# Layer normalisation phases in four groups of four batches, half of the normalising on GpSimd in five of the eight

## The chip, the cores and the metric

The kernel runs on one core of one Trainium2 chip. The metric is the time of one execution in microseconds, measured on the device; lower is better. Times of a profile come from one profiled execution.

## The reference

Input is `x` of 16 batches x 112 rows x 256 features and a context of 16 x 375 x 256, all float32. Four layers follow, each an attention over the context and a feed-forward part with eight experts. Each of the eight parts reads a layer normalisation of the running `x` and is added to it:

```python
def _layernorm(x, axis=-1, eps=1e-05):
    m = jnp.mean(x, axis=axis, keepdims=True)
    v = jnp.var(x, axis=axis, keepdims=True)
    return (x - m) / jnp.sqrt(v + eps)
...
    x = x + _L0_xattn_ref(ctx_1024, _layernorm(x, axis=-1), ctx_1024, ...)
    x = x + _L0_ffn_ref(_layernorm(x, axis=-1), ...)
    x = x + _L1_xattn_ref(_layernorm(x, axis=-1), ctx_1024, ...)
    x = x + _L1_ffn_ref(_layernorm(x, axis=-1), ...)
    x = x + _L2_xattn_ref(_layernorm(x, axis=-1), ctx_1024, ctx_1024, ...)
    x = x + _L2_ffn_ref(_layernorm(x, axis=-1), ...)
    x = x + _L3_xattn_ref(_layernorm(x, axis=-1), ctx_1024, ctx_1024, ...)
    x = x + _L3_ffn_ref(_layernorm(x, axis=-1), ...)
    return x
```

The parts differ: softmax attention with 16 heads of 16 features (layers 0 and 3) or 64 (layer 2), a linear attention (layer 1), and experts chosen by one or two winners or weighted by gates. The change touches only what computes `_layernorm`.

## The kernel before

`x` lies in SBUF as the tile `X` for the whole run: 112 rows on the partitions, 16 batches of 256 features. Each of the eight parts is a phase function that opens with a call of `layernorm_phase` (L95). The calls, by the tag that names their tiles in the trace (the tile of the normalised rows is `a0n_xn` and so on, or `d_xn` in the routers r1, r5 and r7 of the sparse feed-forward parts): a0 and a6 from `narrow_attention_phase` (L833), a2 from `linear_attention_phase` (L1198), a4 from `attention_phase` with heads of 64 (L320), and r1, r3, r5, r7 from `router_phase` (L1552).

`layernorm_phase` is one block of all five engines, with a barrier of all engines at its end (L43), and makes `XT`, the normalised rows turned so that features lie on the partitions. Within it:

- VectorE (DVE) works in two halves of eight batches: `bn_stats` of each batch (L126), `bn_aggr` of each (L129), for both halves; then for each half a `reciprocal` of the eight roots (L133) and eight `tensor_scalar` that subtract the mean and multiply (L138), each 112x256.
- ScalarE (ACT) takes a root of each half's variances (L155) and then copies the eight PSUM banks out to `XT` (L160), each 128x448.
- TensorE (PE) turns each batch in two halves of 128 features (L170), four batches to a bank: for each group of four the four first halves, each waiting for its batch, and then the four second halves. So there are 32 transposes and 8 banks.
- SyncE (SP) runs `fetch`, the DMA of what the phase behind needs: weights, biases, the first context tiles.
- GpSimd (POOL) runs `prepare` where a caller gives one: in a0 and a6 it fills `k`, `q` and `values` (L829 to L831), in a2 one small tile (L1196). `attention_phase` passes a `prepare` as well, but its body does something only with heads of 16, which a4 hasn't. The routers pass none.

The order on each engine is the order of the code; engines meet by semaphores. An instruction that waits holds all that stands behind it on its engine. After the barrier of a4 the first instruction of ScalarE that counts is the cast of a context tile that DMA brings (L467), behind a wait for all weights; ScalarE's casts of the weights and its evacuation of the first projections follow it.

Of the kernel before, what the change touches and what calls it, by code (L numbers as in the profile page):

```python
# [9 lines left out]
ALU = mybir.AluOpType  # L10
ACT = mybir.ActivationFunctionType
AX = mybir.AxisListType

B, S, D = 16, 112, 256
# [4 lines left out]
GT = 4  # L19
G = B // GT  # L20
# [73 lines left out]

def layernorm_phase(nc, tag, X, XT, ident, xn=None, fetch=None, prepare=None):  # L95


    HB = B // 2
    with ExitStack() as st:
        m = Mem(nc, st, tag)  # L100
        stats = m.sb("stats", [S, B, 6])
        mean_var = m.sb("mean_var", [S, B, 2])
        eps = m.sb("eps", [S, 1])
        warm = m.sb("warm", [S, 1])
        std = m.sb("std", [S, B])
        rstd = m.sb("rstd", [S, B])
        xn = m.sb("xn", [S, B, D]) if xn is None else xn
        banks = [m.bank(f"b{i}") for i in range(8)]
        stats_done, mv_done, std_done, rstd_done = (m.sem(n) for n in ("stats", "mv", "std", "rstd"))
        xn_done, turned, evacuated, eps_done = (m.sem(n) for n in ("xn", "turned", "evac", "eps"))  # L110
        with nc.Block() as block:
            if fetch is not None:
                @block.sync
                def _(sp):
                    fetch(sp)

            if prepare is not None:
                @block.gpsimd
                def _(pool):
                    prepare(pool)  # L120

            @block.vector
            def _(dve):
                def statistics(i):
                    for b in range(i * HB, (i + 1) * HB):
                        dve.bn_stats(stats[:, b, :], X[:, b, :]).then_inc(stats_done, 1)  # L126
                    dve.wait_ge(stats_done, (i + 1) * HB)
                    for b in range(i * HB, (i + 1) * HB):
                        dve.bn_aggr(mean_var[:, b, :], stats[:, b, :]).then_inc(mv_done, 1)  # L129

                def invert(i):
                    dve.wait_ge(std_done, i + 1)
                    dve.reciprocal(rstd[:, i * HB:(i + 1) * HB], std[:, i * HB:(i + 1) * HB]).then_inc(rstd_done, 1)  # L133

                def normalise(i):
                    dve.wait_ge(rstd_done, i + 1)
                    for b in range(i * HB, (i + 1) * HB):
                        dve.tensor_scalar(xn[:, b, :], X[:, b, :], mean_var[:, b, 0:1], rstd[:, b:b + 1],  # L138
                                          ALU.subtract, ALU.mult).then_inc(xn_done, 1)

                dve.memset(eps[:, :], LN_EPS).then_inc(eps_done, 1)
                statistics(0)
                statistics(1)
                invert(0)
                normalise(0)
                invert(1)
                normalise(1)

            @block.scalar
            def _(act):  # L150
                act.wait_ge(eps_done, 1)
                act.activation(warm[:, :], eps[:, :], ACT.Sqrt)
                for i in range(2):
                    act.wait_ge(mv_done, (i + 1) * HB)
                    act.activation(std[:, i * HB:(i + 1) * HB], mean_var[:, i * HB:(i + 1) * HB, 1], ACT.Sqrt,  # L155
                                   bias=eps[:, 0:1]).then_inc(std_done, 1)
                for g in range(G):
                    for c in range(DC):
                        act.wait_ge(turned, g * DC + c + 1)
                        act.copy(XT[:, c, g * GW:(g + 1) * GW], banks[g * DC + c][:, 0:GW]).then_inc(evacuated, 1)  # L160
                act.wait_ge(evacuated, G * DC)

            @block.tensor
            def _(pe):
                for g in range(G):
                    for c in range(DC):
                        for t in range(GT):
                            if c == 0:
                                pe.wait_ge(xn_done, g * GT + t + 1)
                            mm = pe.transpose(banks[g * DC + c][:, t * S:(t + 1) * S],  # L170
                                              xn[:, g * GT + t, c * 128:(c + 1) * 128], ident[0:S, 0:S])
                        mm.then_inc(turned, 1)


def attention_phase(nc, tag, X, XT, ident, ctxT, Wq, Wk, Wo, bo, bq=None, bk=None, Wv=None, bv=None,
# [9 lines left out]
    HB = 128 // step  # L185
# [20 lines left out]
    with ExitStack() as st:  # L206
        m = Mem(nc, st, tag)
# [20 lines left out]
        if mask is not None:  # L228
# [11 lines left out]
        projected, evacuated = m.sem("projected"), m.sem("evacuated")  # L240
        scored, least_done, exp_done, inv_done, P_done = (
            m.sem(n) for n in ("scored", "least", "exp", "inv", "P_done"))
        turned, PT_done, av_done, y_done, out_done, x_done = (
            m.sem(n) for n in ("turned", "PT_done", "av", "y", "out", "x_done"))
# [32 lines left out]
        def load_keys(sp, b, u):  # L277
            sp.dma_start(kc[:, u, :, :], ctxT[b].rearrange("(c p) s -> p c s", p=128)).then_inc(kc_in[u], 16)

        def load_rest(sp, b, u):  # L280

            if ctx is not None:
                if not (isinstance(b, int) and b < 2):
                    sp.wait_ge(av_done, H * (b - 1))
                sp.dma_start(v[:, u, :, :], ctx[b].rearrange("(j p) d -> p j d", p=KP)).then_inc(v_in[u], 16)
            if mask is not None:
                src = mask[b] if mask_kind == "per_query" else mask[b].to_broadcast([S, SK])
                sp.dma_start(mask_raw[:, u, :], src).then_inc(mask_in[u], 16)
# [25 lines left out]
        def prepare(pool):  # L314
            if hd == 16:
                pool.memset(wo[:, :, :], 0.0).then_inc(zeroed, 1)
                pool.memset(q[:, :, :, :, :], 0.0).then_inc(zeroed, 1)
                pool.memset(k[:, :, :, :], 0.0).then_inc(zeroed, 1)

        layernorm_phase(nc, tag + "n", X, XT, ident, fetch=fetch, prepare=prepare)  # L320
        P = m.sb("P", [S, 4, SK])
        PT = m.sb("PT", [KP, 2 * HB, KT, S])
        yT = m.sb("yT", [128, 2, NB, S])
# [8 lines left out]
        with nc.Block() as block:  # L332
            @block.sync
            def _(sp):
                def stack(b, u):

                    if not (isinstance(b, int) and b < 2):
                        sp.wait_ge(stack_in[u], 16 * NSLOT * (b // 2) if isinstance(b, int) else (b - u) * (8 * NSLOT))
                        sp.sem_inc(sp_waited, 1)
                    sp.wait_ge(parts_made, QK * (b + 1))  # L340
                    rows = lambda d: d[u].rearrange("n (c p) s -> p n c s", p=128)
                    for part in range(2):
                        sp.dma_start(rows(q_dram)[:, part], q_parts[:, part, :, :]).then_inc(parts_out, 16)
# [36 lines left out]
                stack(B - 1, 1)  # L380
# [1929 lines left out]
```

## Time and profile before

| what | value |
|---|---|
| three runs | 3030.3, 3033.42, 3039.56 us; median 3033.42 |
| the profiled execution | 3027.69 us |
| its span | 3026.1 us, 59465 instructions |
| PE busy | 2436.0 us (81%) |
| DVE busy | 1298.1 us (43%) |
| ACT busy | 1126.1 us (37%) |
| POOL busy | 953.0 us (31%) |
| all `tensor_scalar` of L138 | 128, in eight phases of 16 |

Busy time is a share of the whole span; what a phase costs is read in the timeline of that phase, from its first `bn_stats` to its last copy of L160.

### The profile page before, as it was taken

How to read it: one execution, taken by the hardware profiler on the slowest of the kernel's cores; microseconds unless marked ns; L12 is line 12 of the kernel's file. 1: busy time of each engine (PE TensorE's matmuls, PEld its weight loads, DVE VectorE, ACT ScalarE, POOL GpSimd, SP SyncE). 2: the span in 40 equal slices, each digit the busy share in tenths (PEclk: the TensorE clock that was granted, in tenths of full speed). 3: DMA queues.
4: the chain of work that ended last, by engine and by line, in shares of the span. 5: the costliest groups of instructions: out<-in, count | busy, mean ns of one | idle time of the engine just before them, and what ended most of it. 6: DMA issues, size and time to landing. Idle time of an engine off the chain costs nothing. (4 is left out here: it accounts for less than half of the span.)

```text
span 3026.1 us, 59465 instructions
## 1 busy us (share of the span) xinstructions
PE 2436.0 (81%) x20918; PEld 1782.1 (59%) x20918; DVE 1298.1 (43%) x3094; ACT 1126.1 (37%) x2531; POOL 953.0 (31%) x1201
## 2 busy tenths in 40 slices
PE   3998499499999999879799899899865962899653
PEld 1555289366777776646466666666634851555432
DVE  4555401445554555435344444444451224544432
ACT  1455143333333333121455555555421211455411
POOL 4332200344333344100345444544333025222022
PEclk9899599799999999979899999999976986999867
DMA  6552198200000000000564565565404633332045
GB/s 168 102 104 63 43 324 309 97 17 12 7 12 12 12 12 2 2 11 18 137 124 98 98 129 103 94 125 109 75 15 153 219 127 88 72 67 62 6 128 164
DMA packets 334154, 266.26 MB, mean 88 GB/s; under 512 B 128376, under 2 KB 314624, under 8 KB 333952
## 3 DMA queue, kind: packets, MB, share of 16 engines
q1 hardware_dynamic: 324112, 237.70, 32.8%
q0 software_dynamic: 9840, 25.70, 2.5%
q8 instruction: 146, 2.39, 0.4%
q14 instruction: 56, 0.46, 0.1%
HBM read 181.19 MB, written 57.61 MB: 79 GB/s over the span
## 5 line engine op out<-in xcount | busy, mean ns | idle before, releaser
L1292 POOL TENSOR_TENSOR a_kp<-a_kp 125x512 f16<-125x512 f32 x192 | 219.0, 1158 | 394.7 <-ACT a_kp L1321 384.5
L993 DVE TENSOR_REDUCE a_mx<-a_s 112x2 f32<-112x750 f32 x256 | 234.5, 935 | 224.3 <-PE a_s L1050 224.2
L1420 PE MATMUL a_u<-a_wkf,a_kc 128*125 128x512 f16 x1152 | 263.0, 389 | 27.5 <-issue 20.0
L395 POOL TENSOR_SCALAR a_P<-a_P,a_inv 112x375 f32<-112x375 f32 x256 | 151.7, 593 | 357.3 <-DVE a_inv L555 355.8
L550 DVE CUSTOM_DVE_ANT_0 a_masked<-a_s,a_mask_add 112x375 f32<-112x375 f32 x256 | 140.1, 547 | 281.4 <-PE a_s L661 279.8
L475 ACT ACTIVATE a_P<-a_masked,a_least 112x375 f32<-112x375 f32 x256 | 156.0, 609 | 200.9 <-DVE a_least L550 198.6
L1420 PEld LDWEIGHTS a_u<-a_wkf,a_kc 128*125 128x125 f16 x1152 | 158.7, 140 | 121.3 <-issue 36.0
L945 ACT ACTIVATE a_PT<-a_x 125x672 f32<-125x672 f32 x256 | 186.8, 730 | 100.4 <-PE a_x L1063 99.0
L2115 ACT ACTIVATE f_h<-f_h,f_b1s 128x128 f32<-128x128 f32 (+1 forms) x294 | 116.4, 397 | 240.2 <-PE f_h L2089 227.5
L1342 DVE TENSOR_SCALAR a_kp<-a_u 125x512 f32<-125x512 f32 x192 | 128.5, 689 | 179.4 <-PE a_u L1420 146.8
L561 DVE COPY a_PT<-a_t 125x336 f32<-125x336 f32 x256 | 129.1, 504 | 153.2 <-PE a_t L670 153.2
L1321 ACT CAST a_kp<-a_kp 125x512 f16<-125x512 f32 x192 | 117.8, 618 | 193.7 <-DVE a_kp L1342 193.7
L2089 PE MATMUL f_h<-f_xT,f_w 128*128 128x128 f32 (+1 forms) x1176 | 183.7, 313 | 0.1
L2100 PE MATMUL f_o<-f_w,f_h 128*128 128x256 f32 x756 | 174.1, 381 | 0.0
L2089 PEld LDWEIGHTS f_h<-f_xT,f_w 128*128 128x128 f32 x1176 | 165.1, 197 | 9.7 <-ACT f_h L2115 0.4
L634 PE MATMUL a_p<-a_kc,a_wk 128*128 128x375 f16 x768 | 143.8, 325 | 29.0 <-ACT a_raw L456 29.0
L2043 POOL DMA_DIRECT2D expert_rows<-f_y x63 | 38.0, 602 | 385.7 <-DVE f_y L2132 385.3
L2132 DVE COPY f_y<-f_o 128x256 f32<-128x256 f32 x84 | 35.7, 425 | 279.5 <-PE f_o L2100 279.5
L2100 PEld LDWEIGHTS f_o<-f_w,f_h 128*128 128x128 f32 x756 | 141.6, 192 | 17.3
L637 PE MATMUL a_p<-a_wv,a_kc 128*125 128x512 f16 x576 | 140.8, 383 | 0.0
L661 PE MATMUL a_s<-a_k,a_q 128*112 128x375 f16 x512 | 129.2, 336 | 9.1 <-DMA a_k<-k_parts 8.9
L670 PEld LDWEIGHTS a_t<-all_ident,a_P 112*125 112x125 f32 x768 | 118.9, 192 | 17.8 <-POOL a_P L395 2.2
(316 smaller groups left out, 4822.2 us busy)
## 6 DMA issues: line engine op xcount, KB each, us to landing
f_w<-in_L_ffn_W SPq DMA_DIRECT2D x42, 1024.0 KB, 6.6
a_kc<-in_ctxT SPq DMA_DIRECT2D x64, 375.0 KB, 5.0
k_parts<-a_k_parts SPq DMA_DIRECT2D x32, 750.0 KB, 7.3
a_k<-k_parts SPq DMA_DIRECT2D x32, 750.0 KB, 11.3
f_w<-in_L_ffn_ew SPq DMA_DIRECT2D x42, 512.0 KB, 3.8
a_k<-a_k_parts SPq DMA_DIRECT2D x192, 93.8 KB
a_q<-q_parts SPq DMA_DIRECT2D x64, 224.0 KB, 4.6
f_w<-in_L_ffn_W SPq DMA_DIRECT2D x42, 256.0 KB, 3.0
```

The lines of the kernel that those rows point to most:

```text
L395: pool.tensor_scalar(P[:, h % 4, :], P[:, h % 4, :], inv[:, u, h:h + 1], 1.0, ALU.mult, ALU.mult).then_inc(P_done, 1)
L475: act.activation(P[:, h % 4, :], src, ACT.Exp, bias=least[:, u, h:h + 1], scale=-1.0, accum_out=total[:, u, h:h + 1]).then_inc(exp_done, 1)
L550: dve.tensor_tensor_reduce(masked[:, h % 2, :], s_bank[h % 2][0:S, 0:SK], mask_add[:, u, :], 1.0, 3e38, ALU.add, ALU.min, least[:, u, h:h ...
L634: mm = pe.matmul(out[:, 0:SK], wk16[:, z, i, c * 128:(c + 1) * 128], kc16[:, u, x, i, :], **flags)
L637: mm = pe.matmul(out[0:KP, 0:VN], kc16[:, u, x, i, c * KP:(c + 1) * KP], wv16[:, z, i, w * VN:(w + 1) * VN], **flags)
L661: mm = pe.matmul(s_bank[h % 2][0:S, 0:SK], q[:, u, NPASS - 1 - n, h, :], k[:, u, h * KH // H, :], start=n == 0, stop=n == NPASS - 1)
L945: act.activation(PT[:, p % 4, :, :], x_bank[0:KP, :, 0:KT * S], ACT.Exp).then_inc(exp_done, 1)
L993: dve.tensor_reduce(mx[:, b % 2, 2 * pair:2 * pair + 2], s_bank[p % 2][0:S, :, 0:SK], AX.X, ALU.max).then_inc(max_done, 1)
L1292: pool.tensor_tensor(kp16[:, LO, j, w * 512:(w + 1) * 512], kp[:, n % 4, :], kp16[:, HI, j, w * 512:(w + 1) * 512], ALU.subtract).then_inc ...
L1420: mm = pe.matmul(out[0:KP, 0:512], kc16[:, u, a, c, j * KP:(j + 1) * KP], wt[:, z, c, w * 512:(w + 1) * 512], start=n_mm == 0, stop=n_mm = ...
L2089: mm = pe.matmul(h_bank[n % R][:, 0:TS], w1[:, s, c, f * 128:(f + 1) * 128], xT[:, s, c, :], start=c == 0, stop=c == DC - 1)
L2100: mm = pe.matmul(o_bank[n % R][:, 0:D], h[:, s, f, t * 128:(t + 1) * 128], w2[:, s, f, :], start=f == 0, stop=f == FC - 1)
```

## The change

The statistics, inversion and normalising go in four groups of four batches instead of two halves of eight. VectorE computes statistics one group ahead of the normalising. In a phase without `prepare` VectorE normalises the first two batches of each group and GpSimd the other two; with `prepare`, VectorE normalises all four. ScalarE takes the root of group g before it copies the banks of group g - 2. PE waits for VectorE's or GpSimd's semaphore according to the batch. `attention_phase` passes its `prepare` only with heads of 16, so that in a4 GpSimd shares in the normalising; r1, r3, r5 and r7 do as well, a0, a2 and a6 don't.

```diff
+    own = GT if prepare is not None else 2
...
+        def normalise(eng, b, done):
+            eng.tensor_scalar(xn[:, b, :], X[:, b, :], mean_var[:, b, 0:1], rstd[:, b:b + 1],
+                              ALU.subtract, ALU.mult).then_inc(done, 1)
...
+            @block.gpsimd
+            def _(pool):
+                if prepare is not None:
                     prepare(pool)
+                else:
+                    for g in range(G):
+                        pool.wait_ge(rstd_done, g + 1)
+                        for t in range(own, GT):
+                            normalise(pool, g * GT + t, xn_pool)
...
+                def statistics(g):
+                    for b in range(g * GT, (g + 1) * GT):
                         dve.bn_stats(stats[:, b, :], X[:, b, :]).then_inc(stats_done, 1)
+                    dve.wait_ge(stats_done, (g + 1) * GT)
+                    for b in range(g * GT, (g + 1) * GT):
                         dve.bn_aggr(mean_var[:, b, :], stats[:, b, :]).then_inc(mv_done, 1)
...
+                def invert(g):
+                    dve.wait_ge(std_done, g + 1)
+                    dve.reciprocal(rstd[:, g * GT:(g + 1) * GT], std[:, g * GT:(g + 1) * GT]).then_inc(rstd_done, 1)
+                    dve.wait_ge(rstd_done, g + 1)
+                    for t in range(own):
+                        normalise(dve, g * GT + t, xn_dve)
...
                 statistics(0)
-                statistics(1)
-                invert(0)
-                normalise(0)
-                invert(1)
-                normalise(1)
+                for g in range(1, G):
+                    statistics(g)
+                    invert(g - 1)
+                invert(G - 1)
...
+                for g in range(G):
+                    act.wait_ge(mv_done, (g + 1) * GT)
+                    act.activation(std[:, g * GT:(g + 1) * GT], mean_var[:, g * GT:(g + 1) * GT, 1], ACT.Sqrt,
+                                   bias=eps[:, 0:1]).then_inc(std_done, 1)
+                    if g >= 2:
+                        evacuate(g - 2)
+                evacuate(G - 2)
+                evacuate(G - 1)
...
+                            if c == 0 and t < own:
+                                pe.wait_ge(xn_dve, g * own + t + 1)
+                            elif c == 0:
+                                pe.wait_ge(xn_pool, g * (GT - own) + t - own + 1)
...
-        layernorm_phase(nc, tag + "n", X, XT, ident, fetch=fetch, prepare=prepare)
+        layernorm_phase(nc, tag + "n", X, XT, ident, fetch=fetch, prepare=prepare if hd == 16 else None)
```

## Rows read from the trace of the kernel before

**Rows 1.** Timeline of r1: start us, us, engine, line, operation, count, idle before and releaser.
```profile
309.97 0.43 DVE L126 BATCH_NORM_STATS2 r1n_stats<-all_X 112x6 f32<-112x256 f32 x1 [1.20 <-PEq L43]
...
313.27 2.68 DVE L126 BATCH_NORM_STATS2 r1n_stats<-all_X 112x6 f32<-112x256 f32 x8
...
316.55 0.17 DVE L133 RECIPROCAL r1n_rstd<-r1n_std 112x8 f32<-112x8 f32 x1
...
316.75 2.68 DVE L138 TENSOR_SCALAR d_xn<-all_X,r1n_mean_var,r1n_rstd 112x256 f32<-112x256 f32 x8
...
317.22 6.65 PE L170 MATMUL r1n_b<-all_ident,d_xn 112*128 112x112 f32 x32 [8.92 <-DVE d_xn L138]
...
323.16 0.53 ACT L160 COPY all_XT<-r1n_b 128x448 f32<-128x448 f32 x1 [0.21 <-PE r1n_b L170]
323.90 0.53 ACT L160 COPY all_XT<-r1n_b 128x448 f32<-128x448 f32 x1 [0.22 <-PE r1n_b L170]
```

**Rows 2.** Timeline of r3, then stretches: us, PE busy (count), granted clock, DMA share, GB/s.
```profile
1282.25 2.71 DVE L126 BATCH_NORM_STATS2 r3n_stats<-all_X 112x6 f32<-112x256 f32 x8
...
1294.94 0.97 ACT L160 COPY all_XT<-r3n_b 128x448 f32<-128x448 f32 x2 [0.17 <-PE r3n_b L170]
...
1291.00:1292.00 1.00, 1.00 (x7) 0.50 0.00 0
...
1294.00:1295.00 1.00, 0.99 (x9) 1.00 0.00 0
```

**Rows 3.** Timeline of a2.
```profile
568.17 2.71 DVE L126 BATCH_NORM_STATS2 a2n_stats<-all_X 112x6 f32<-112x256 f32 x8
...
579.86 1.99 ACT L160 COPY all_XT<-a2n_b 128x448 f32<-128x448 f32 x4 [0.21 <-PE a2n_b L170]
```

**Rows 4.** Timeline of a0.
```profile
16.57 10.10 POOL L829 MEMSET a_k<- 128x12000 f16 x1 [14.82 <-POOLq L43]
...
19.95 2.68 DVE L126 BATCH_NORM_STATS2 a0n_stats<-all_X 112x6 f32<-112x256 f32 x8
...
23.43 13.90 DVE L138 TENSOR_SCALAR a0n_xn<-all_X,a0n_mean_var,a0n_rstd 112x256 f32<-112x256 f32 x8
...
26.61 6.22 POOL L830 MEMSET a_q<- 128x7168 f16 x1
...
26.87 0.45 PE L170 MATMUL a0n_b<-all_ident,a0n_xn 112*128 112x112 f32 x1 [26.87 <-DVE a0n_xn L138]
32.77 2.79 POOL L831 MEMSET a_values<- 125x3072 f32 x1
...
35.77 5.59 PE L170 MATMUL a0n_b<-all_ident,a0n_xn 112*128 112x112 f32 x30 [2.29 <-DVE a0n_xn L138]
...
37.47 2.68 DVE L138 TENSOR_SCALAR a0n_xn<-all_X,a0n_mean_var,a0n_rstd 112x256 f32<-112x256 f32 x8
...
41.01 0.97 ACT L160 COPY all_XT<-a0n_b 128x448 f32<-128x448 f32 x2 [0.18 <-PE a0n_b L170]
```

**Rows 5.** Timeline of a6.
```profile
2540.24 2.68 DVE L138 TENSOR_SCALAR a6n_xn<-all_X,a6n_mean_var,a6n_rstd 112x256 f32<-112x256 f32 x8
...
2542.33 2.08 ACT L160 COPY all_XT<-a6n_b 128x448 f32<-128x448 f32 x4 [0.21 <-PE a6n_b L170]
```

**Rows 6.** GpSimd operations by line: min/median/max ns; the last from the groups: busy us, mean ns.
```profile
L395 POOL TENSOR_SCALAR a_P<-a_P,a_inv x256: 591/592/602, 1515.7 to 2198.3; 112x375 f32<-112x375 f32 x128
...
L921 POOL TENSOR_SCALAR a_bqT<-a_bqT x2: 277/386/496, 42.9 to 2545.3; 128x2 f32<-128x2 f32 x2
...
L1564 POOL TENSOR_TENSOR all_X<-all_X,d_xn 112x256 f32<-112x256 f32 x16 | 11.0, 723 | 23.3 <-SPq L1559 23.3
```

**Rows 7.** Timeline of a4 and what follows.
```profile
1446.84 0.43 DVE L126 BATCH_NORM_STATS2 a4n_stats<-all_X 112x6 f32<-112x256 f32 x1 [0.99 <-PEq L43]
...
1460.77 0.53 ACT L160 COPY all_XT<-a4n_b 128x448 f32<-128x448 f32 x1 [0.21 <-PE a4n_b L170]
...
1462.95 0.82 ACT L467 CAST a_kc<-a_kc 128x750 f16<-128x750 f32 x1 [1.65 <-DMA a_kc<-in_ctxT]
```

More of the change, by code:

```diff
@@ L95, in layernorm_phase @@
 def layernorm_phase(nc, tag, X, XT, ident, xn=None, fetch=None, prepare=None):
-    HB = B // 2
+    own = GT if prepare is not None else 2
     with ExitStack() as st:
@@ L109, in layernorm_phase @@
         stats_done, mv_done, std_done, rstd_done = (m.sem(n) for n in ("stats", "mv", "std", "rstd"))
-        xn_done, turned, evacuated, eps_done = (m.sem(n) for n in ("xn", "turned", "evac", "eps"))
+        xn_dve, xn_pool, turned, evacuated, eps_done = (m.sem(n) for n in ("xn_dve", "xn_pool", "turned", "evac", "eps"))
+        def normalise(eng, b, done):
+            eng.tensor_scalar(xn[:, b, :], X[:, b, :], mean_var[:, b, 0:1], rstd[:, b:b + 1],
+                              ALU.subtract, ALU.mult).then_inc(done, 1)
         with nc.Block() as block:
@@ L115, in _ @@
                     fetch(sp)
-            if prepare is not None:
-                @block.gpsimd
-                def _(pool):
+            @block.gpsimd
+            def _(pool):
+                if prepare is not None:
                     prepare(pool)
+                else:
[3 more added lines that the diff above has]
+                            normalise(pool, g * GT + t, xn_pool)
             @block.vector
@@ L123, in _ @@
             def _(dve):
-                def statistics(i):
-                    for b in range(i * HB, (i + 1) * HB):
+                def statistics(g):
+                    for b in range(g * GT, (g + 1) * GT):
                         dve.bn_stats(stats[:, b, :], X[:, b, :]).then_inc(stats_done, 1)
-                    dve.wait_ge(stats_done, (i + 1) * HB)
-                    for b in range(i * HB, (i + 1) * HB):
+                    dve.wait_ge(stats_done, (g + 1) * GT)
+                    for b in range(g * GT, (g + 1) * GT):
@@ L129, in statistics @@
                         dve.bn_aggr(mean_var[:, b, :], stats[:, b, :]).then_inc(mv_done, 1)
[L131 to L139, printed above, removed]
+                def invert(g):
[4 more added lines that the diff above has]
+                        normalise(dve, g * GT + t, xn_dve)
@@ L141, in _ @@
                 dve.memset(eps[:, :], LN_EPS).then_inc(eps_done, 1)
                 statistics(0)
-                statistics(1)
-                invert(0)
-                normalise(0)
-                invert(1)
-                normalise(1)
+                for g in range(1, G):
+                    statistics(g)
+                    invert(g - 1)
+                invert(G - 1)
             @block.scalar
             def _(act):
-                act.wait_ge(eps_done, 1)
-                act.activation(warm[:, :], eps[:, :], ACT.Sqrt)
@@ L153, in _, with evacuate @@
[L153 to L157, printed above, removed]
+                def evacuate(g):
                     for c in range(DC):
@@ L160, in _ @@
                         act.copy(XT[:, c, g * GW:(g + 1) * GW], banks[g * DC + c][:, 0:GW]).then_inc(evacuated, 1)
+                act.wait_ge(eps_done, 1)
+                act.activation(warm[:, :], eps[:, :], ACT.Sqrt)
+                for g in range(G):
[6 more added lines that the diff above has]
+                evacuate(G - 1)
                 act.wait_ge(evacuated, G * DC)
@@ L167, in _ @@
                         for t in range(GT):
-                            if c == 0:
-                                pe.wait_ge(xn_done, g * GT + t + 1)
+                            if c == 0 and t < own:
+                                pe.wait_ge(xn_dve, g * own + t + 1)
+                            elif c == 0:
+                                pe.wait_ge(xn_pool, g * (GT - own) + t - own + 1)
                             mm = pe.transpose(banks[g * DC + c][:, t * S:(t + 1) * S],
```

## Prediction

> **What bounds the kernel now.** The page's first part comes first: PE is by far the busiest engine, so a stretch in which PE stands still costs its full length. The eight layer normalisations are such stretches: each stands alone between two barriers of all engines, and what follows it starts only when its last ScalarE copy is done. I call them by their tags: a0, r1, a2, r3, a4, r5, a6, r7. I read each in the timeline, counted from the first `bn_stats` of VectorE (DVE).
>
> r1 [rows 1] is the plain case. Eight `bn_stats` and eight `bn_aggr` take 313.27 to 316.55 = 3.28 us, 2.68 of it the `bn_stats`; the aggregates are 0.07 each. A `reciprocal` is followed by the first normalising `tensor_scalar` 0.20 us later. Eight of those take 316.75 + 2.68; one lasts 0.41 us and follows the last by 0.324 us. The first comes at 6.78 us, the sixteenth ends at 12.28. PE then transposes 32 times in 6.65 us without a gap; the last copy ends at 323.90 + 0.53, that is at 14.46. a4 repeats the pattern to the same end. In r3, r5 and r7 the last copy ends at 13.66 (1294.94 + 0.97 - 1282.25 in r3, which stands for the three): the granted clock of PE is 0.50 at first and 1.00 in the last microsecond [rows 2]. 1.00 is the 2.4 GHz level and 0.50 the 1.2 GHz level. a2 ends at 579.86 + 1.99 - 568.17 = 13.68 [rows 3].
>
> a0 and a6 differ. GpSimd fills three large tiles there (10.10, 6.22 and 2.79 us). DVE's `bn_stats` run at their usual pace beside the first (8 in 2.68), but the first `tensor_scalar`, issued at 23.43, has its result only when PE starts at 26.87, 0.2 us after the first memset ends at 26.67. The second and third likewise come out at the ends of the second and third memset: PE's long run starts at 35.77 [rows 4]. So a DVE `tensor_scalar` and a GpSimd instruction exclude each other, and a `bn_stats` doesn't care. In a0 DVE then needs until 37.47 + 2.68 = 40.15 and the copies until 41.01 + 0.97 = 41.98 [rows 4]; in a6 2540.24 + 2.68 = 2542.92 and 2542.33 + 2.08 = 2544.41 [rows 5].
>
> **The change part by part.** First the units. Statistics of four batches instead of eight: 3.28 less four spacings (1.30) and four aggregates (0.28) = 1.70 us. Inversion and n normalisations: 0.20 + 0.324 n. The tail from the last normalised batch to the last copy, when PE isn't behind: 0.06 to wake, five transposes at 0.186 (four in 0.74, the spacing of the last copies [rows 1]), 0.2 to drain, 0.03 + 0.53 for the copy = 1.75 us; at the higher clock half the transposing, about 1.3.
>
> *a0 and a6, four batches on DVE: a loss.* DVE is in order. It now comes to its first `tensor_scalar` at about 3.6 us, while the first memset runs on to 26.67, and there it stands: the statistics of groups 2 and 3, which before lay under that memset, are queued behind it. The three releases stay where they are, since the memsets set them. The fourth `tensor_scalar` starts at 23.43 + 13.90 - 0.41 - 4 x 0.324 = 35.62 [rows 4] and frees DVE at 35.95. Then statistics 1.70, group 1 1.50, statistics 1.70, group 2 1.50, and group 3 with 0.20 + 3 x 0.324 + 0.41: the last ends at 43.93 in place of 40.15, 3.78 us later. With the tail of 1.75 the last copy ends at 45.68 instead of 41.98: +3.7. In a6 2546.70 + 1.75 against 2544.41: +4.0. At the shorter tail it is 3.2 and 3.6. Both delays pass on whole, as a barrier follows. The stretch that hid the work (the memset) has lost its content, and nothing else is late enough to cover.
>
> *a2, four on DVE, a short memset: a small loss.* Statistics twice, 3.40; then 1.50, 1.70, 1.50, 1.70, 1.50, and 0.20 + 0.97 + 0.41: the last ends at 12.88 instead of the 12.28 of r1 (four inversions instead of two, four drains instead of two). With 1.75 the end is 14.6 against 13.68: +0.95, or +0.5 at the higher clock.
>
> *r1, r3, r5, r7, two on DVE and two on GpSimd: a gain.* The first normalisation comes at 3.60 instead of 6.78. DVE: 3.40, +0.85 = 4.25, 5.95, 6.80, 8.50, 9.35, and the last ends at 10.28. The price of one on GpSimd isn't in the trace: its one-scalar form on 375 columns takes 592 ns and on 2 columns 277 at the least, so by the straight line 256 columns take 492; `tensor_tensor` on 112x256 takes 723 and is my upper bound [rows 6]. I take 492, the same operation. Groups 2 and 3 on GpSimd run from 8.70 to 10.7. PE, with 1.49 us a group, is behind then: group 2 to 10.7, group 3 to 12.2, last copy at 12.95. How much the exclusion costs in each group isn't shown for two short instructions; from 0 to full alternation. The overlap needed is only a part of each: a `tensor_scalar` follows the memset's end in 0.2 us, and GpSimd's data part is 254 x 0.845 = 215 ns. I take 0.3 to 0.8 us over the phase, of which PE's backlog hides half: end at 13.2. That is 1.25 less in r1 and 0.45 less in each of r3, r5 and r7: 2.6 together. With 723 ns the last batch comes at 11.6 and the end is at 13.4, 0.8 less gain over the four.
>
> *a4: nothing.* ScalarE's first cast of the next block waits for the DMA of `kc` until 1462.95, while the last copy ended at 1460.77 + 0.53 = 1461.30, 14.46 after the first `bn_stats` [rows 7]: an earlier end only waits longer for what SP fetches beside it, and there is some 0.6 us of slack before a later end costs.
>
> ScalarE's order (root of group g ahead of the copies of group g - 2) costs nothing: root 2 is done by about 6.3, before the banks of group 0 hurt, and the copies were never the bound (0.53 each against 0.74 of PE). One more semaphore to clear is within the barrier.
>
> Sum: +3.7 + 4.0 + 0.95 - 1.25 - 1.35 = **+6.0 us**. Against the profiled execution that is 3027.69 + 6.0 = 3033.7 (1.6 us of it lie outside the span); the median of the runs, 3033.42, is 5.7 above that execution, so the forecast is **3039.4**. Bounds: losses 7.3 to 8.7, gains down to below zero (next part) and up to 7.8.
>
> One rule speaks against the change. The Trainium skill, "SBUF — State Buffer", section "Who interferes with whom", says that a GpSimd instruction and a VectorE instruction in a 2-port mode, which a float32 `tensor_scalar` from SBUF to SBUF can enter, hold one pair of ports for the whole instruction and block the other fully. The stall behind the memsets agrees with it. By it two short ones alternate in full, which is the first rival; by my rows they overlap in part.
>
> **The rivals.**
>
> *Full alternation: slower.* If each `tensor_scalar` of either engine shuts out the other for its whole length, two pairs cost 0.41 + 0.49 each: DVE leaves a group after 1.31 instead of 0.65, the statistics of group 3 end at 9.82, and the eight instructions of groups 2 and 3 take 10.0 to 13.7. The end is at 15.45: +1.0 in r1, +1.8 in each of three, +0.4 in a4. With 8.65 of losses the sum is +15.4, 3048.8. For it: the memset rows; against it: only waits on very long instructions are shown. It decides when more than about 1.3 us of a phase goes into waiting. Chance 0.18 (with sums from +9). A change that in effect leaves all the work in one line ("doesn't do what it says") is this case too.
>
> *The clock rises early: no loss.* If PE, which starts 3.2 us earlier, is at 1.00 for the last groups, the end is at 10.7 + 1.2 = 11.9: 2.5 less in r1, 1.75 in three, 7.8 together, and the three losses are 7.3: -0.5, 3032.9. For it: r3, r5, r7 and a2 rise within their run of transposes. Against: r1 and a4 don't, and PE now has gaps between groups, where before it had none. The matmuls that follow each phase hang on the same level, either way. Chance 0.12.
>
> *The gain is real and nothing is lost in a0 and a6.* It would need the second half's statistics to pass a waiting instruction on DVE. Sum about -3; it takes a shift of later loops besides to be faster by 0.3%. Chance 0.05.
>
> **How the numbers follow.** The forecast's own case (+2 to +9) has 0.65. About 0.3% is what a measurement of this kernel can tell from no change, 9.1 us. Slower by more: the alternation and the upper edge of my own case, 0.22. Faster by more: 0.05, for the third rival and what a rhythm of later loops may do. Within: 0.73. The runs before spread from 3030.3 to 3039.56, so the range is 3030 to 3049: from the case of the early clock with a low median up to full alternation.
>
> **What would show it.** In a0 and a6 after: the first `tensor_scalar` issued near 3.6 us, statistics of groups 2 and 3 behind the last memset, last copy 3.7 to 4.0 us later. In a2 the end at 14.2 to 14.6. In r1, first transpose at 4.0 and last copy near 13.2; GpSimd's `tensor_scalar` near 0.49 us and DVE's spacing between 0.33 and 0.8. In a4 the cast still waits for the DMA until the same time after the barrier. The prediction is wrong if GpSimd's instruction costs over 0.73 us, if DVE's two stand still behind it, or if the a0 and a6 delay meets a cover that I don't see.

## The result

The changed kernel takes 3072.74 us in the median against 3036.2 in the same comparison: a ratio of 1.0111, 95% interval 1.0087 to 1.0136. In a later comparison on another chip, beside the experiments, it was 1.0091 (1.0071 to 1.0110; 3074.6 against 3046.2). It is slower by about 1%, 28 to 34 us, where 6 us were forecast. One execution of the version that normalises on ScalarE took 4348.61 us at a granted clock of 0.551, and it is left out of that version's ratio.

The head of the page of the changed kernel, to set beside the table of before:

```profile
span 3072.7 us, 59497 instructions
...
PE 2488.6 (81%) x20918; PEld 1801.3 (59%) x20918; DVE 1299.8 (42%) x3070; ACT 1131.8 (37%) x2547; POOL 1005.9 (33%) x1241
```

A stretch that can be compared from kernel to kernel is a block: from the first `bn_stats` of a phase to the first instruction of the next block (the cast of `ident16`, the `memset` of a PSUM bank or the cast of `XT`), which stands in each timeline. The stretch behind a phase runs from the end of its block to the first `bn_stats` of the next phase, and the rest is the sum of these stretches.

| profile | a0 | r1 | a2 | r3 | a4 | r5 | a6 | r7 | sum | rest |
|---|---|---|---|---|---|---|---|---|---|---|
| before, four profiles | 26.0-26.4 | 14.7-15.5 | 14.6-15.4 | 14.7-15.3 | 14.7-15.5 | 14.7-15.3 | 25.9-26.2 | 14.7-15.2 | 141.3-142.7 | 2868-2886 |
| after | 30.2 | 17.0 | 15.7 | 17.0 | 17.0 | 17.5 | 30.1 | 17.0 | 161.5 | 2894 |
| after, again | 30.2 | 17.0 | 15.7 | 17.0 | 17.0 | 17.5 | 30.1 | 17.0 | 161.5 | 2888 |

(The four of before are the first profile, two of the same code taken later, and one with a hidden instruction more, below.) The blocks are 20 us longer and repeat to 0.1 us; that is six to seven tenths of the result. The rest varies by 11 us in three profiles of one kernel (2868, 2879, 2879), and the first profile of before has the lowest.

What happened in r1, to set beside [rows 1]; timeline of the changed kernel, columns as there:

```profile
320.91 0.43 DVE L135 BATCH_NORM_STATS2 r1n_stats<-all_X 112x6 f32<-112x256 f32 x1 [1.20 <-PEq L43]
...
324.53 0.90 DVE L112 TENSOR_SCALAR d_xn<-all_X,r1n_mean_var,r1n_rstd 112x256 f32<-112x256 f32 x2
324.60 5.27 POOL L112 TENSOR_SCALAR d_xn<-all_X,r1n_mean_var,r1n_rstd 112x256 f32<-112x256 f32 x4 [34.42 <-DVE r1n_rstd L142]
...
325.35 1.39 DVE L135 BATCH_NORM_STATS2 r1n_stats<-all_X 112x6 f32<-112x256 f32 x4
...
327.25 0.90 DVE L112 TENSOR_SCALAR d_xn<-all_X,r1n_mean_var,r1n_rstd 112x256 f32<-112x256 f32 x2
...
330.03 5.00 POOL L112 TENSOR_SCALAR d_xn<-all_X,r1n_mean_var,r1n_rstd 112x256 f32<-112x256 f32 x4 [0.16 <-DVE r1n_rstd L142]
...
333.91 0.53 ACT L159 COPY all_XT<-r1n_b 128x448 f32<-128x448 f32 x1 [0.21 <-PE r1n_b L182]
...
335.09 1.19 PE L182 MATMUL r1n_b<-all_ident,d_xn 112*128 112x112 f32 x5 [0.66 <-POOL d_xn L112]
...
336.32 0.53 ACT L159 COPY all_XT<-r1n_b 128x448 f32<-128x448 f32 x1 [0.21 <-PE r1n_b L182]
```

The first normalisation comes where it was forecast, 3.62 us after the first statistics (324.53 - 320.91), and VectorE's two take 0.90 for 0.73. But GpSimd's run without a pause and the phase waits for them: the last transposes start at 335.09, released by GpSimd, and the last copy ends at 336.85, 15.9 us after the start instead of 13.2. The eight of r1 by themselves, from the view of the line (min/median/max ns):

```profile
L112 POOL TENSOR_SCALAR d_xn<-all_X,r1n_mean_var,r1n_rstd x8: 1212/1232/1369, 324.6 to 333.8; 112x256 f32<-112x256 f32 x8
```

The median of all 40 in the profile is 1233 ns, the mean 1275. In r1 the four that have no `tensor_scalar` of VectorE beside them still take 1212 to 1219 ns.

a0, to set beside [rows 4]:

```profile
17.25 10.10 POOL L841 MEMSET a_k<- 128x12000 f16 x1 [15.49 <-POOLq L43]
...
17.32 1.41 DVE L135 BATCH_NORM_STATS2 a0n_stats<-all_X 112x6 f32<-112x256 f32 x4
...
20.94 15.77 DVE L112 TENSOR_SCALAR a0n_xn<-all_X,a0n_mean_var,a0n_rstd 112x256 f32<-112x256 f32 x4
...
27.28 6.22 POOL L842 MEMSET a_q<- 128x7168 f16 x1
...
36.63 1.39 DVE L135 BATCH_NORM_STATS2 a0n_stats<-all_X 112x6 f32<-112x256 f32 x4
...
38.53 1.38 DVE L112 TENSOR_SCALAR a0n_xn<-all_X,a0n_mean_var,a0n_rstd 112x256 f32<-112x256 f32 x4
...
41.74 1.38 DVE L112 TENSOR_SCALAR a0n_xn<-all_X,a0n_mean_var,a0n_rstd 112x256 f32<-112x256 f32 x4
...
43.25 1.38 DVE L112 TENSOR_SCALAR a0n_xn<-all_X,a0n_mean_var,a0n_rstd 112x256 f32<-112x256 f32 x4
...
45.91 0.53 ACT L159 COPY all_XT<-a0n_b 128x448 f32<-128x448 f32 x1 [0.21 <-PE a0n_b L182]
```

VectorE stands at the first `tensor_scalar` from 20.94 until the three memsets let it through, one at a time; only then, at 36.63, do the statistics of group 2 run. Groups 1 and 2 are normalised 3.2 us apart (38.53 and 41.74), since the statistics of group 3 lie between them, and group 3 follows 1.5 us behind. The last copy ends at 46.44, 29.1 after the start, against 25.3 before. In a6, to set beside [rows 5], PE works in pieces with gaps of 1 us ahead of groups 1 and 2, as in a0:

```profile
2567.58 1.39 DVE L135 BATCH_NORM_STATS2 a6n_stats<-all_X 112x6 f32<-112x256 f32 x4
...
2573.17 3.67 PE L182 MATMUL a6n_b<-all_ident,a6n_xn 112*128 112x112 f32 x16 [1.05 <-DVE a6n_xn L112]
...
2574.20 1.38 DVE L112 TENSOR_SCALAR a6n_xn<-all_X,a6n_mean_var,a6n_rstd 112x256 f32<-112x256 f32 x4
```

### The profile page after: what moved, and what is told of

Read it like the earlier page. It is cut to its first block and busy times, and to the rows that moved or that the text cites. A ratio compares the mean times of both kernels' runs of the same rounds, so it can differ in the third digit from the quotient of the medians.

```text
span 3072.7 us, 59497 instructions
## 1 busy us (share of the span) xinstructions
PE 2488.6 (81%) x20918; PEld 1801.3 (59%) x20918; DVE 1299.8 (42%) x3070; ACT 1131.8 (37%) x2547; POOL 1005.9 (33%) x1241
## 5 line engine op out<-in xcount | busy, mean ns | idle before, releaser
L573 DVE COPY a_PT<-a_t 125x336 f32<-125x336 f32 x256 | 129.1, 504 | 153.2 <-PE a_t L682 153.2
L646 PE MATMUL a_p<-a_kc,a_wk 128*128 128x375 f16 x768 | 144.4, 326 | 29.1 <-ACT a_raw L468 29.1
```

The source lines that it names most:

```text
L573: dve.tensor_copy(PT[:, h % (2 * HB), :, :], t_bank[h % 2][0:KP, 0:KT * S].rearrange("p (j s) -> p j s", j=KT)).then_inc(PT_done, 1)
L646: mm = pe.matmul(out[:, 0:SK], wk16[:, z, i, c * 128:(c + 1) * 128], kc16[:, u, x, i, :], **flags)
```

## The experiments

**First question: what makes the blocks longer, and the rest.** The two profiles that stood beside each other at first, 3026.1 and 3072.7 us, showed 20 us more in the blocks and 26 us more in the rest, most of it behind a0 (+6), r1 (+4), a2 (+4) and a6 (+11), each time with PE at a lower granted clock. The theory of the clock, which the expectations name, is that PE's work in short pieces leaves its granted clock at 0.50, and that the next stage starts with it. Four kernels split the change.

VectorE alone, four groups everywhere:

```diff
-    own = GT if prepare is not None else 2
+    own = GT
```

> The changed kernel with VectorE normalising all four batches of every group and GpSimd none; the four groups stay. In the changed kernel a GpSimd normalisation lasts 1275 ns, and the last copy of r1, r3, a4, r5 and r7 comes 15.9 us after the first statistics. If GpSimd's price is what makes these five phases late, they end here as a2 does, at 14.8: some 1.1 less each, 5 to 6 us less than the changed kernel, and about 30 us more than the kernel before. The stretches behind a0 and a6 stay as long as in the changed kernel (274 and 319 us) whichever theory holds for them, as long as it lies in the four groups; if GpSimd were behind those stretches too (rival), they fall to 268 and 308.

Measured: 1.0072 (1.0044 to 1.0100), 3067.7 us. The interval overlaps that of the changed kernel, so the gain is read in the blocks. Timeline of r1:

```profile
315.57 1.41 DVE L130 BATCH_NORM_STATS2 r1n_stats<-all_X 112x6 f32<-112x256 f32 x4
...
329.77 0.53 ACT L154 COPY all_XT<-r1n_b 128x448 f32<-128x448 f32 x1 [0.21 <-PE r1n_b L177]
```

The last copy ends at 330.30, 14.7 us after the start instead of 15.9. r1, r3, a4, r5 and r7 have blocks of 15.8 instead of 17.0 to 17.5, as expected; sum 155.0. So in the changed kernel GpSimd's help costs 1.2 to 1.7 us in each of the five phases compared with no help at all. The stretch behind a6 stayed at 318. That behind a0 was 268.5, as the rival had it; it varies by more than this in the kernel before, so it decides nothing.

The change in the five phases alone, with the halves of before in a0, a2 and a6:

```diff
+    phase = layernorm_in_groups if prepare is None else layernorm_in_halves
```

> The change only in the phases without prepare (r1, r3, a4, r5, r7); a0, a2 and a6 keep the two halves of the kernel before. Theory of the clock: the stretches behind a0, a2 and a6 return to 268, 700 and 308 us and those three phases to 25.3, 13.6 and 25.0. What stays is the five phases, 1.4 to 2.3 us more each, about 10 us, and perhaps 0 to 5 behind r1: 10 to 15 us over the kernel before. If the long stretches come from something that all versions of the new code share (rival), it is 30 us over.

Measured: 1.0055 (1.0034 to 1.0075), blocks 152.5 (+10.7); the phases are as expected, the time is 17 us (10 to 23) for 10 to 15. But the stretches behind a0, a2 and a6 did not return: 273.7, 707.0 and 316.6 us, with the old code in these phases. My theory, that only those three phases' gaps lengthen what is behind them, was at least incomplete.

The complement:

```diff
+    phase = layernorm_in_halves if prepare is None else layernorm_in_groups
```

> The complement: the four groups only in a0, a2 and a6, the kernel before in the other five. Theory of the clock: those phases cost 3.8, 1.2 and 4.1 us more and the stretches behind them 6, 4 and 11 us more, together about 30 us over the kernel before, and this with the last experiment adds up to the changed kernel. The rival, that only the phases themselves are longer, says 9 us over.

Measured: 1.0053 (1.0034 to 1.0072), some 16 us, half of the 30 expected; blocks 151.1 (+9.4). Its one profile does have the long stretches, 275.4, 704.5 and 315.8 us behind a0, a2 and a6, so the 30 came from setting it beside the first profile of before. The two halves of the change add up: 17 and 16 us beside 28 to 34 for the whole.

Filler work for PE in the gaps of a0, a2 and a6 of the changed kernel:

```diff
                         mm.then_inc(turned, 1)
+                    if prepare is not None and g < G - 1:
+                        for n in range(8):
+                            pe.transpose(banks[(g + 1) * DC + n // GT][:, (n % GT) * S:(n % GT + 1) * S],
+                                         xn[:, g * GT, 0:128], ident[0:S, 0:S])
```

> The changed kernel, but in a0, a2 and a6 PE fills the gap behind each of the first three groups with eight more transposes, into the banks of the next group, which are overwritten after. They lie where PE waits for VectorE, so the phases stay at 29.1, 14.8 and 29.1 us. If the granted clock stays at 0.50 because PE now works in short pieces there (theory of the clock), it rises here within or soon after the phase, and the stretches behind a0, a2 and a6 fall back towards 268, 700 and 308 us: about 20 us less than the changed kernel. If the gaps have nothing to do with it, the time is that of the changed kernel.

Measured: 1.0070 (1.0037 to 1.0102), 3067.5 us, inconclusive by itself against 1.0091 and 1.0111; about 20 us less were expected. In the profile the stretch behind a6 fell from 318 to 312.7, those behind a0 and a2 didn't fall (272.8, 708.1).

**Second question: is the first profile typical, and does waiting cost more than itself?** The kernel before once more, unchanged:

> The kernel before, unchanged, profiled once more. In the experiment with the halves kept in a0, a2 and a6 the stretches behind these phases took 275, 708 and 318 us, against 268, 700 and 308 in the first profile of the kernel before, with the same code there. If the first profile was a lucky execution (theory now), this one shows about 275, 708 and 318 us too, with the granted clock at 0.50 for tens of us more. If the long stretches belong to the change, it shows 268, 700 and 308 again.

It took 3039.07 us, 2879 in the rest: 273.0 behind a0, 700.4 behind a2, 312.5 behind a6. So for a0 and half of a6 the theory of a lucky first profile holds; behind a2 the unchanged code keeps its 700.

A later end of every block, with nothing else changed:

```diff
                 normalise(1)
+                for b in range(B):
+                    dve.bn_stats(stats[:, b, :], X[:, b, :]).then_inc(stats_done, 1)
+                dve.wait_ge(stats_done, 2 * B)
```

> The kernel before, but VectorE repeats its sixteen first statistics at the end of every layer normalisation, results unused, so that each of the eight blocks ends 3.0 to 3.8 us later (in a0 and a6 3.4) with all other work as before: 27 us of idle time for PE. In the runs so far the kernels were slower by about 1.7 times what their phases were longer. If a us of waiting costs PE more than itself, by the clock it is granted afterwards, this is 40 to 50 us over the kernel before; if it costs only itself, 27; in the latter case the surplus of the changed kernel lies elsewhere.

Measured: 1.0110 (1.0078 to 1.0142), about 34 us; the blocks are 171.0, 29.3 us more. The interval, 24 to 43 us, holds both the waiting alone and up to nearly half as much again, so this one doesn't decide; a cost of 1.7 per us of waiting (50 us) is excluded.

**Third question: what is wrong with GpSimd's price?** One column of scalars instead of two:

```diff
-            eng.tensor_scalar(xn[:, b, :], X[:, b, :], mean_var[:, b, 0:1], rstd[:, b:b + 1],
-                              ALU.subtract, ALU.mult).then_inc(done, 1)
...
+                            pool.tensor_scalar(xn[:, b, :], X[:, b, :], rstd[:, b:b + 1], 1.0,
+                                               ALU.mult, ALU.mult).then_inc(xn_pool, 1)
```

> The changed kernel, with GpSimd's instruction reading one column of scalars instead of two: it multiplies by the inverse root and leaves out the subtraction of the mean, for eight of sixteen batches in r1, r3, a4, r5 and r7. The prediction priced it at 492 ns from the one-column form on 375 columns; the two-column form measured 1275. If the second column is what costs, this one takes about 0.5 us, VectorE is held less, and the five phases end near the 13.2 us forecast instead of 15.9: 10 to 13 us less than the changed kernel. If GpSimd's price comes from running beside VectorE (rival), it stays near 1.2 us and the time stays.

Its line in the trace, and r1 of it:

```profile
L130 POOL TENSOR_SCALAR d_xn<-all_X,r1n_rstd x8: 497/534/616, 327.3 to 334.2; 112x256 f32<-112x256 f32 x8
```

```profile
323.63 0.43 DVE L137 BATCH_NORM_STATS2 r1n_stats<-all_X 112x6 f32<-112x256 f32 x1 [1.20 <-PEq L43]
...
327.25 0.82 DVE L112 TENSOR_SCALAR d_xn<-all_X,r1n_mean_var,r1n_rstd 112x256 f32<-112x256 f32 x2
327.31 1.09 POOL L130 TENSOR_SCALAR d_xn<-all_X,r1n_rstd 112x256 f32<-112x256 f32 x2 [34.75 <-DVE r1n_rstd L144]
...
332.53 0.82 DVE L112 TENSOR_SCALAR d_xn<-all_X,r1n_mean_var,r1n_rstd 112x256 f32<-112x256 f32 x2
332.59 2.12 POOL L130 TENSOR_SCALAR d_xn<-all_X,r1n_rstd 112x256 f32<-112x256 f32 x4 [1.54 <-DVE r1n_rstd L144]
...
336.50 0.53 ACT L161 COPY all_XT<-r1n_b 128x448 f32<-128x448 f32 x1 [0.21 <-PE r1n_b L184]
```

532 ns in the median of all 40 instead of 1233, and the last copy ends at 337.03, 13.4 us after the first statistics at 323.63, in all five phases; 13.2 was forecast. The ratio is 1.0045 (1.0029 to 1.0060), 14 us in place of 28, and 12.5 us less in the blocks. So the form of GpSimd's instruction is what costs, not its running beside VectorE, and the model of the phase was right but for that price. Two things differ between the forms, though: the second column of scalars is gone, and the subtraction has become a multiplication. No run takes them apart. In `tensor_tensor` a subtraction isn't dear on GpSimd: to float16, 876 ns on 375 columns and 394 on 112 (medians of L389 in the kernel before), by the straight line some 660 on 256, where an addition in float32 takes 723. That speaks for the column, but isn't a measurement of this instruction. VectorE is delayed by 0.09 us for a pair here (0.82 for 0.73, the time of a pair in the version with ScalarE below).

**Fourth question: is there a surplus at all?** Every edited kernel had more than its blocks account for, 3 to 14 us and some 7 in the middle, in most of them no more than the run's own interval. Three controls:

The kernel before against itself:

> The kernel before against itself, for the size of a difference that means nothing. From one block's first statistics to the next block's first instruction, summed over the eight phases, the kernel before has 141.4 and 141.9 us in two profiles; the rest of the program took 2868 and 2879 us. Every edited kernel so far had 2890 to 2898 us in that rest, whatever was edited, and its median is 2 to 16 us more than its blocks account for. If that surplus is chance, this comparison may show one as well, of up to 10 us; if it comes from edited code, this one shows 0 within 5 us.

0.9996 (0.9980 to 1.0011), blocks 141.9, rest 2879.

The kernel before with one hidden instruction more (the diff of the later end, with one `bn_stats` instead of sixteen):

> The kernel before with one more statistics instruction at VectorE's end of each layer normalisation, 0.4 us that lie under the last copies of ScalarE (VectorE is done 1.4 to 2.2 us before them), so that the blocks keep 141 to 142 us. Theory: the surplus in the rest is not tied to the length of the blocks, and this kernel shows some 7 us more than the one before, though nothing waits for the new instruction. Rival: the surplus is a consequence of what the blocks do to PE's clock; then this one shows 0 within 5 us.

0.9993 (0.9978 to 1.0008), blocks 142.7. My theory falls: an edit as such costs nothing.

The changed kernel beside them:

> The changed kernel once more, beside the others on this chip. Its blocks sum to 161.6 us against 141.9, 20 us more. If only the blocks count, it is 20 us slower here; with the surplus of the other edited kernels 25 to 30; in its first comparison it was 34.

1.0091 (1.0071 to 1.0110), 22 to 34 us, of which the blocks are 19.8 (161.5 against 141.7). So there is a surplus of 2 to 14 us, 8 at the centre.

**Fifth question: where the surplus is.** In all four profiles of kernels with unchanged blocks, a6 ends with PE at 1.00 and the next 18 us stay there; in nine of the ten profiles of edited kernels taken so far PE is at 0.50 for the first 13 to 35 us behind a6. The one exception is that with filler work in the gaps. Among the nine is the kernel that keeps the halves of before in a6, so gaps within a6 can't be the only way to this state. Hence a6 alone, with the groups and without filler:

```diff
+        phase = layernorm_in_groups if tag == "a6" else layernorm_phase
```

> The kernel before with the four groups, all on VectorE, in a6 alone. Theory of the clock: a6's block is 4 us longer, PE works in it in pieces of 2 us with gaps of 1 us and is granted 0.50 to its end; behind it 0.50 goes on for 13 us or more, and the stretch to r7 takes 315 to 318 us instead of 307 to 313: 8 to 10 us over the kernel before. Rival (the surplus has nothing to do with a6's gaps): 4 us over, the stretch at 307 to 313.

and with eight filler transposes in each of its three gaps (the diff of the filler above, for a6 alone; it puts eight behind each of the first three groups):

> The same with eight filler transposes of PE in each of the three gaps of a6. Theory of the clock: the granted clock rises within a6 to 1.00 and is 1.00 when the next block starts, the stretch to r7 takes 307 to 313 us and the kernel is 3 to 5 us over the kernel before, 4 to 6 less than without filler. Rival: no difference between the two.

Measured: 1.0049 (1.0028 to 1.0071) without filler, 15 us where 8 to 10 were expected, and 1.0022 (1.0002 to 1.0043) with it, 7 us. The two were run side by side; worked out from their single times (10 and 12), the means differ by 7.2 us, with an interval of 2 to 13. The stretches of PE around the end of a6's block (us, PE busy with its count, granted clock, DMA share, GB/s; the first row is the block's last 3 us), first before and after, then without and with filler:

```profile
2542.30:2545.30 3.00, 1.44 (x12) 0.92 0.00 0
2545.30:2557.30 12.00, 8.60 (x23) 1.00 0.14 31
```

```profile
2575.30:2578.30 3.00, 1.54 (x9) 0.50 0.00 0
2578.30:2590.30 12.00, 10.03 (x15) 0.50 0.00 0
```

```profile
2560.00:2563.00 3.00, 1.50 (x9) 0.50 0.00 0
2563.00:2575.00 12.00, 10.07 (x15) 0.50 0.00 1
```

```profile
2575.10:2578.10 3.00, 1.45 (x16) 1.00 0.00 0
2578.10:2590.10 12.00, 8.62 (x23) 1.00 0.14 32
```

With the same code behind the block, PE gets through 23 instructions in the first 12 us where it ended at 1.00, and through 15 where it ended at 0.50. The stretch from a6 to r7 is 315.8 without filler and 307.1 with it (before has 307.0 to 312.8). The block of a6 is 29.6 with filler and 30.1 without. So the 8.7 us in this stretch are of the size of the difference between the two kernels, though the profiled execution with filler was by chance the longer one (3059.1 us; 287.7 behind a0). Wherever a6 is in groups on VectorE without filler, PE ends it at 0.50 (six profiles), and with filler at 1.00 (two). This part of the surplus is shown: with work in pieces, PE went into the next stage at 0.50, and filling the gaps brought the 1.00 and the time back.

It isn't the whole account. With the halves of before in a6 and the change in the five other phases, PE reached 1.00 within the block, and fell to 0.50 as the next began, for 17 us:

```profile
2567.90:2570.90 3.00, 1.46 (x13) 1.00 0.00 0
2570.90:2582.90 12.00, 10.07 (x16) 0.51 0.00 0
```

What took the clock down there, with the block's code unchanged, isn't known.

Last, a version that does better. ScalarE normalises, as scale and bias of an activation, in two of each four batches, and in a0 and a6 in all:

```diff
+                    dve.scalar_tensor_tensor(shift[:, group], mean_var[:, group, 0], -1.0, rstd[:, group],
+                                             ALU.mult, ALU.mult).then_inc(shifted, 1)
...
+                def scale(g):
+                    act.wait_ge(shifted, g + 1)
+                    for b in range(g * GT + own, (g + 1) * GT):
+                        act.activation(xn[:, b, :], X[:, b, :], ACT.Identity, bias=shift[:, b:b + 1],
+                                       scale=rstd[:, b:b + 1]).then_inc(xn_act, 1)
```

> ScalarE takes over what the change gave to GpSimd, as scale and bias of one activation each, the bias being minus mean times inverse root from VectorE: two of each four batches in r1, a2, r3, a4, r5 and r7, all four in a0 and a6, where it isn't held by GpSimd's memsets as VectorE's tensor_scalar is. The six phases should end at 12 to 13 us, and a0 and a6 at 19 to 20, when the last memset is done, instead of 25.3. Phases 16 to 20 us shorter than before in sum, so about 3025 where the kernel before takes 3045; if only the end of the memsets or ScalarE's own queue binds (rival), no more than 5 to 10 us less.

Measured: 0.9971 (0.9953 to 0.9988), 3040.0 against 3045.0, some 9 us less (4 to 14) where 20 were expected: the only version clearly faster than both. Its line and a0:

```profile
L170 ACT ACTIVATE a0n_xn<-all_X,a0n_shift,a0n_rstd x16: 585/592/612, 20.9 to 30.3; 112x256 f32<-112x256 f32 x16
```

```profile
16.96 10.10 POOL L851 MEMSET a_k<- 128x12000 f16 x1 [15.21 <-POOLq L43]
...
20.85 2.08 ACT L170 ACTIVATE a0n_xn<-all_X,a0n_shift,a0n_rstd 112x256 f32<-112x256 f32 x4
...
28.82 2.09 ACT L170 ACTIVATE a0n_xn<-all_X,a0n_shift,a0n_rstd 112x256 f32<-112x256 f32 x4
...
30.80 1.92 ACT L158 COPY all_XT<-a0n_b 128x448 f32<-128x448 f32 x4
...
33.01 2.66 POOL L853 MEMSET a_values<- 125x3072 f32 x1
36.48 0.22 DVE L1040 CAST a_ident<-all_ident 112x112 f16<-112x112 f32 x1 [9.95 <-PEq L43]
```

ScalarE isn't held by the memset and turns out four batches in 2.08 us; the copies are done at 32.7, and the next block begins at 36.48, after GpSimd's last memset (33.01 + 2.66 = 35.67): the block is 19.5 us instead of about 26. The six others end at 13.8 instead of the 12 to 13 expected, with blocks of 14.7 to 14.9, no gain. In r1 ScalarE's last two normalisations begin at 316.19, though their bias was ready at 315.25: two copies stand before them in its queue. The blocks are 13.6 us shorter in sum, which the interval of the time just holds.

The same in a0 and a6 only, with the halves elsewhere:

> The two halves of the kernel before in six phases, and in a0 and a6 only the groups with all normalising on ScalarE. These two blocks should be 19.4 us as in the last such experiment instead of 26.1, bound by the last memset, all others as before: 13 us less in the blocks. Without a surplus 13 us faster than the kernel before (0.4%), with one of 7 only 6.

0.9987 (0.9971 to 1.0003), 4 us less and within the noise; blocks 129.1, the stretch behind a6 at 318. And this version with twenty filler transposes behind PE's last in a0 and a6:

> The version with ScalarE normalising in a0 and a6, with twenty filler transposes behind PE's last in these two blocks, 3.7 us that lie under GpSimd's memsets. The blocks stay at 19.4 us. Theory of the clock: PE is granted 1.00 at the start of the next stage, the stretch behind a6 falls from 318 to 307 to 313 us, and the kernel is 8 to 13 us faster than the one before (0.3 to 0.4%). Rival: it stays at 1 to 4 us faster.

1.0044 (1.0025 to 1.0064), 13 us slower than before, though the filler did its work in a6: PE at 1.00 behind it and the stretch at 307.0. The loss is elsewhere: 722.0 us behind a2, against 699 to 702 in the unchanged kernels and 710.6 in the version without filler. It isn't explained by the clock: the mean granted clock there is 0.960, against 0.959 without filler. What it is stays open.

## Why the prediction failed, point by point

- *Units of VectorE, the tail, PE's pace*: right. The first normalisation was forecast at 3.60 and came at 3.62; statistics of four were forecast at 1.70 and take 1.70 to 1.73, and with a GpSimd instruction at about the forecast price the five phases ended at 13.4 for 13.2.
- *a0 and a6*: right, +3.7 and +4.0 forecast for their ends, +3.8 and +4.1 measured (+4.0 and +4.2 in the blocks). The cover that was lost is the one named: statistics under the memset. *a2*: +0.95 forecast, +1.1 at the end of the phase.
- *The price of one normalisation on GpSimd*: the step that failed. "I take 492, the same operation" rested on a form with one column and one without; my upper bound of 723 was wrong as well. It is 1233 ns in the median and 1275 in the mean. I had given the second column and the subtraction no price on GpSimd and had no row for either. The sign of being wrong that I had named, over 0.73 us, came true. At 1.25 us eight of them are 10 us in a row from 3.6 us on, longer than the whole phase was to last after that: r1 got +1.5 at its end instead of -1.25, r3, r5 and r7 +2.3 instead of -0.45. Over the four that is 11 us between forecast and result.
- *a4 costs nothing*: right for an end that comes earlier: ScalarE's first cast starts 15.8 us after the first `bn_stats` with the end at 13.4 (one column) and with the end at 13.7 (before, again). But the end came 1.5 us later, beyond the slack of 0.6: the cast starts at 16.9 instead of 16.1, and the block, which ends with a `memset` of VectorE, grew by the whole 1.5 to 17.0. The stretch behind it kept its 745.
- *Full alternation*: that rival's size (15 us in sum, an end at 15.45 for the measured 15.9) was nearest, but by luck, since its mechanism isn't what happened. In r1 two of VectorE's instructions take 0.90 while GpSimd is inside one of 1.37 us that began 0.07 after them. Waits of that kind came to 0.17 us for a pair, where full alternation needs 0.49 and more. The rule of the Trainium skill that I weighed ("SBUF — State Buffer", "Who interferes with whom": the pair is held for the whole instruction) agrees with the memsets (VectorE's `tensor_scalar` stands until they end, for up to 6.5 us in the changed kernel), but not with these short instructions; the measurement decides.
- *The clock*: I carried it as a gain (PE starts earlier) and wrote that what follows hangs on it "either way", but gave that no price. It was a loss: 3 to 11 us behind a6 in the profiles (315.6 and 318.3 for 307.0 to 312.8). The gaps that I named as the argument against my own rival were a thing to cost: filling them in a6 gave back 2 to 13 us.
- *The sum*: losses of 8.65 were forecast for a0, a6 and a2, and 9.2 measured in the blocks; gains of 2.6 turned into a further loss of about 10 in five phases; together 20 in the blocks. What remains is 2 to 14 us by the later comparison, 14 at the centre of the first, and of it only the part behind a6 has a cause that is shown.

What stays open: behind a2, unchanged blocks have 698.6 to 702.1 us in four profiles and the edited kernels 704 to 711 in all profiles but three (701.1 with the later end, 701.9 with groups and filler in a6 alone, 722.0 above), also where a2's own block was as before. In all of them the granted clock dips to 0.50 several times in that long loop for some us, for longer in the slower ones (the mean granted clock of the stretch is 0.971 to 0.976 for the unchanged blocks, 0.970 and 0.973 in the first two exceptions, 0.959 to 0.966 in the others). What sets off the dips wasn't found. Behind a0 the dips differ between profiles of the same code (267 to 280 us for the unchanged blocks, 269 and 273 for the changed kernel), so a0 says nothing on the change.

## What to carry to other kernels

An instruction moved to another engine must be priced in its own form there, with every operand: on GpSimd the form that subtracts one column of scalars and multiplies by another took 1233 ns where the form with one column took 532, while VectorE does the dearer form in 0.41 us. Splitting work into finer groups for an earlier start also takes it out of a cover it had (here a memset under which statistics ran, and behind which the in-order VectorE then stood). And PE's idle gaps just ahead of a dense stage can be paid again behind the barrier, if they leave the clock low: look at the granted clock in the first us of the next stage, and try filler work in the gaps. Measure it, too: in a6 it paid, and in the last version above it made the kernel slower.

## What the runs showed of the hardware

- `tensor_scalar` of 112x256 float32 on GpSimd: 1233 ns in the median for subtract and multiply with two columns of scalars, 532 for two multiplications with one column and a constant; the straight line through the forms with one column and without had given 492.
- The same work as an activation with scale and bias columns: 592 ns on ScalarE, one every 0.50 us (four in 2.08), also while GpSimd's memset runs, behind which VectorE's `tensor_scalar` of the changed kernel stands for up to 6.5 us.
- VectorE's two `tensor_scalar` beside GpSimd's: 0.90 us for the pair against 0.73 beside none; beside the form with one column 0.82.
- Behind a6, PE gets through 23 instructions of the same code in 12 us when it comes in at 1.00, and through 15 at 0.50.
- One kernel unchanged spread over 3032 to 3055 us on one chip; half a dozen runs don't give its median to better than some us, and one profile isn't its typical execution.
